# A fused attention and retrieval layer: probabilities scaled in place by ScalarE, Silu as one activation, and another order of the steady turn

## The reference

```python
scores = jnp.einsum('bhqd,bhkd->bhqk', qh, kh) * inv_sqrt_d
scores = jnp.where(causal, scores, jnp.finfo(scores.dtype).min)
attn = jax.nn.softmax(scores, axis=-1)
out = jnp.einsum('bhqk,bhkd->bhqd', attn, vh)
...
h = act(jnp.einsum('btd,cd->btc', hidden_states, W_up) + b_up)      # act is silu
h = jnp.einsum('btc,pc->btp', h, W_down) + b_down
q = jnp.einsum('btp,rp->btr', h, W_q)
...
sim = jnp.einsum('pbthn,hkpn->pbthk', q, keys)
scores, idx = lax.top_k(sim, K_PER_HEAD)
...
z = jnp.einsum('btd,bthkd->bthk', h, de)
z = act(z * jax.nn.softmax(sc, axis=-1))
out = jnp.einsum('bthk,bthkd->btd', z, ue)
...
x = x + jnp.tanh(g_xattn[0]) * _L0_xattn_ref(_layernorm(x, axis=-1), ...)
x = x + jnp.tanh(g_ffn[0]) * _L0_ffn_ref(_layernorm(x, axis=-1), ...)
```

## Time and profile before

| | |
|---|---|
| median of 3 executions | 1224.88 us (1223.29 to 1225.61) |
| the profiled execution, its own time | 1223.2 us |
| its span in the profile | 1221.5 us |
| TensorE matmuls busy | 1147.4 us, 94% |
| VectorE busy | 1074.5 us, 88% |
| ScalarE busy | 703.6 us, 58% |
| GpSimd busy | 332.6 us, 27% |
| mean granted TensorE clock | 0.98 |

### The profile page before, as it was taken

How to read it: one execution, slowest core, us unless ns; L and a number is a source line. 1 busy time by engine, 2 the same in 40 slices (tenths; PEclk the granted TensorE clock), 3 DMA queues, 4 the chain that set the end, 5 groups by cost and what they waited for, 6 DMA issues and landing times. The chain is left out here.

```text
span 1221.5 us, 47601 instructions
## 1 busy us (share of the span) xinstructions
PE 1147.4 (94%) x19004; PEld 1025.1 (84%) x19004; DVE 1074.5 (88%) x4298; ACT 703.6 (58%) x2474; POOL 332.6 (27%) x149
## 2 busy tenths in 40 slices
PE   6876999999999999999999999999999999999857
PEld 4766888888888888888889888888888888888856
DVE  3479999999999999999999999999999999998983
ACT  4656655556666555666556576655557665555310
POOL 4131233321233332123333212333321233331020
PEclk9987999999999999999999999999999999999978
DMA  8034655654565565456456435655644564654544
GB/s 220 12 102 116 151 110 124 151 130 120 125 151 111 123 151 128 115 132 148 101 135 151 128 115 132 151 87 146 151 122 119 135 151 87 147 144 114 127 120 79
DMA packets 304947, 154.52 MB, mean 127 GB/s; under 512 B 282735, under 2 KB 295895, under 8 KB 296535
## 3 DMA queue, kind: packets, MB, share of 16 engines
q1 hardware_dynamic: 304727, 151.47, 51.4%
HBM read 79.62 MB, written 4.72 MB: 69 GB/s over the span
## 5 line engine op out<-in xcount | busy, mean ns | idle before, releaser
L360 POOL TENSOR_TENSOR rstd<-veps,minus_half 128x1 f32<-128x1 f32 x32 | 67.9, 2123 | 709.9 <-DVE veps L831 709.9
L1162 PE MATMUL bank<-ue,coef 128*128 128x256 f32 x1024 | 228.5, 382 | 0.7 <-ACT coef L421 0.7
L1162 PEld LDWEIGHTS bank<-ue,coef 128*128 128x128 f32 x1024 | 193.5, 192 | 26.2 <-ACT coef L421 0.8
L928 PEld LDWEIGHTS bank<-z,hot_rT 128*128 128x128 bf16 x2048 | 155.7, 96 | 35.7 <-issue 23.1
L949 PE MATMUL bank<-uc,hot_r 128*128 128x32 bf16 x6144 | 162.0, 177 | 21.8 <-issue 16.8
L461 ACT ACTIVATE P<-bank,smax 128x64 f32<-128x64 f32 x512 | 152.2, 349 | 47.1 <-DVE smax L656 47.1
L949 PEld LDWEIGHTS bank<-uc,hot_r 128*128 128x128 bf16 x6144 | 158.0, 96 | 24.1 <-issue 20.4
L928 PE MATMUL bank<-z,hot_rT 128*128 128x32 bf16 x2048 | 164.9, 177 | 11.6 <-DVE picked L628 11.5
L928 PE MATMUL bank<-zl,hot_rT 128*128 128x32 bf16 x2048 | 163.7, 177 | 1.3 <-issue 1.2
L928 PE MATMUL bank<-zll,hot_rT 128*128 128x32 bf16 x2048 | 163.6, 177 | 0.0
L928 PEld LDWEIGHTS bank<-zl,hot_rT 128*128 128x128 bf16 x2048 | 156.5, 96 | 1.4 <-issue 1.3
(11 more groups left out here) (142 smaller groups left out, 2292.3 us busy)
## 6 DMA issues: line engine op xcount, KB each, us to landing
hot_rT<-expert_rows SPq DMA_DIRECT2D x64, 1024.0 KB, 6.2
xt<-in_x SPq DMA_DIRECT2D x32, 128.0 KB, 2.5
out<-x1k SPq DMA_DIRECT2D x32, 128.0 KB, 2.2
ct<-in_ctx SPq DMA_DIRECT2D x32, 64.0 KB, 2.3
ue<-in_L_ffn_up_embed SPq DMA_DIRECT2D x1, 2048.0 KB, 12.6
z<-in_L_ffn_W_up SPq DMA_DIRECT2D x1, 1024.0 KB, 8.0
expert_rows<-r_h SPq DMA_DIRECT2D x64, 8.0 KB, 1.8
hot_r<-hot_rT SPq DMA_TRANSPOSE x64, 6.9
```

What stands on the lines that cost most here:

```text
L360: nc.gpsimd.tensor_tensor(rstd[:, :], veps[:, :], minus_half[:, :], ALU.pow).then_inc(S["rstd_ok"], 1)
L928: last = mm(bank[:, 32 * (q - 16 * k):32 * (q - 16 * k) + 32], hot_rT[:, q, :], part.rearrange("r (h q) c -> r h q c", h=2)[:, :, q, :], s ...
L1162: last = mm(bG0[:, 0:DM], coef[:, c, :, :].rearrange("r h q -> r (h q)"), ue[:, c, :], start=(c == 0), stop=(c == C - 1))
```

## The change

Five things change together.

1. ScalarE scales the probabilities in place by `rinv`, with 16 new activations of 128x64 (`normed_probs`, L473). `r_wide`, its transpose and `rT` go, and `oT` becomes a plain copy (L821). The probabilities are transposed only after the scaling.
2. In steady turns Silu is one ScalarE activation with the bias in it (`up_silu`, L426), four of 128x128 per half. The tanh, and VectorE's product, go there. Silu is in another activation table than exp, so the built program has two table loads in each such turn.
3. In steady turns TensorE runs hidden layer, `dense(0)`, `dense(1)`, similarities and `dense(2)` ahead of the transposes of the probabilities, and the attended values behind `scatter(1)`. ScalarE's list follows.
4. The transposes of the normalised inputs move from the end of the products with the output rows to behind the 12th of the 16, those of the next tile's input with them.
5. The keys' two products use different rows and different banks, so `k_diag` is written by 8 activations of 128 columns and not by 4 of 256. VectorE's order of gather products, maxima and sums changes, and `dif` moves down a little.

The diff, cut to its core:

```diff
-                    WdT[:, 4 * g:4 * g + 4, :], 0.5
+                    WdT[:, 4 * g:4 * g + 4, :], 1.0
...
+                def up_silu(n):
+                    Fw.wait(f"up_pe{n}")
+                    Fw.free("hid_pe")
+                    for m in range(4):
+                        c = 4 * n + m
+                        last = nc.scalar.activation(up_act[:, c, :], bS[n][:, 128 * m:128 * m + 128], ACT.Silu,
+                                                    bias=bup_sb[:, c:c + 1])
+                    last.then_inc(S[f"act{n}"], 1)
...
                 def exps(half):
                     A.wait(f"max{half}")
-                    if Fw and Ct:
-                        Fw.wait("act1")
                     A.free("rinv_ok")
...
+                def normed_probs(half):
+                    for n in range(8):
+                        h = 8 * (n // 4) + 4 * half + n % 4
+                        last = nc.scalar.activation(P[:, h, :], P[:, h, :], ACT.Copy, scale=rinv[:, h:h + 1])
+                    last.then_inc(S[f"pn{half}"], 1)
...
                 if Fw and Ct:
-                    up_bias(0)
-                    up_tanh(0)
-                if B and Ct and not B.last:
-                    expert_exp(B)
+                    up_silu(0)
...
-                    for h in range(4):
-                        last = nc.scalar.activation(k_diag[:, :, :, h, :], bD[:, 256:512].rearrange("p (a b k) -> p a b k", a=2, b=2),
-                                                    ACT.Copy, scale=head_of[:, h:h + 1])
+                    for a in range(2):
+                        for h in range(4):
+                            last = nc.scalar.activation(k_diag[:, a, :, h, :], (bD, bT)[a][:, 384:512].rearrange("p (b k) -> p b k", b=2),
+                                                        ACT.Copy, scale=head_of[:, h:h + 1])
...
                 if Fw and Ct:
-                    up_bias(1)
-                    up_tanh(1)
+                    up_silu(1)
...
-                if A:
-                    probs_T(0)
-                    probs_T(1)
+                if A:
                     A.wait("rinv_ok")
-                    A.free("rT_pe")
-                    copy(r_wide[:, :, :], rinv[:, :].unsqueeze(2).to_broadcast([128, HEADS, HD]), "rw_ok")
+                    normed_probs(0)
+                    normed_probs(1)
...
-                if Fw:
+                if Fw and Ct:
                     z_copy(0)
                     z_copy(1)
-                if A:
-                    A.wait("rT_pe")
-                    A.free("o_ok")
-                    copy(rT[:, :, :], bD[:, 256:512].rearrange("d (a q) -> d a q", a=2), "rT_sb")
+                    similarities(0)
+                    similarities(1)
+                    z_copy(2)
+                if A:
+                    probs_T(0)
+                    probs_T(1)
...
-                if Fw and Ct:
-                    up_silu(0)
-                    up_silu(1)
                 if Ct:
                     gathered(0)
-                    gathered_sum(0)
                 if A and (Ct or not Fw):
                     scores_max(0)
+                if Ct:
+                    gathered(1)
+                if A and (Ct or not Fw):
                     scores_max(1)
                 if Ct:
-                    gathered(1)
+                    gathered_sum(0)
+                    gathered(2)
                     gathered_sum(1)
-                    gathered(2)
                     gathered(3)
...
                 if A:
-                    A.wait("rT_sb")
+                    A.wait("av_pe")
                     A.free("wo_pe")
-                    nc.vector.tensor_tensor(oT[:, :, :], bD[:, 0:256].rearrange("d (a q) -> d a q", a=2), rT[:, :, :], ALU.mult).then_inc(S["o_ok"], 1)
+                    nc.vector.tensor_copy(oT[:, :, :], bD[:, 0:256].rearrange("d (a q) -> d a q", a=2)).then_inc(S["o_ok"], 1)
...
                 def probs_T(n):
-                    A.wait(f"exp{n}")
+                    A.wait(f"pn{n}")
...
-                if A:
-                    probs_T(0)
+                if Fw:
+                    hidden()
+                if Fw and Ct:
+                    dense(0)
+                    dense(1)
+                    similarity(0)
+                    similarity(1)
+                    dense(2)
...
                 if Ct:
                     scatter(0)
                     scatter(1)
+                if A and Ct:
+                    attended()
+                if Ct:
                     scatter(2)
-                if Ct:
                     scatter(3)
...
                     for c in range(C):
+                        if c == 3 * C // 4:
+                            if A:
+                                normed_T()
+                            if L:
+                                inputs_T(L, 1 - side)
```

More of the change, by code:

```diff
@@ L548, in turn @@
                     exps(1)
-                if B and not Ct:
+                if B and not B.last:
                     expert_exp(B)
@@ L576, in turn @@
                         copy_weights(act, n)
-                if Fw:
+                if Fw and not Ct:
                     similarities(0)
@@ L1024, in output @@
                     last.then_inc(S["wo_pe"], 1)
-                if A:
-                    A.wait("xn_ok")
-                    A.wait_dma_side(f"ctx_in{side}")
-                    if Ct:
-                        Ct.wait("sm_ok")
-                    for k in range(2):
-                        nc.tensor.transpose(bT[:, 128 * k:128 * k + 128], xn1[:, 128 * k:128 * k + 128], ident[:, :])
-                    nc.tensor.transpose(bT[:, 256:384], ct[:, side, :, :].rearrange("p b d -> p (b d)"), ident[:, :]).then_inc(S["xT_pe"], 1)
+                if A and not Fw:
+                    inputs_T(A, side)
                 if Fw and Ct:
```

137 lines of the change are left out of this document (75 added, 62 removed), and 2 rows, old and new, of the table S.

## The result

The median of the changed kernel is 1392.37 us (1391.75 to 1392.47, 4 runs), against 1224.09 us (1221.12 to 1225.61) for the kernel before on the same chip. The ratio is 1.1381, with a 95% interval of 1.1361 to 1.1402. The direction and the ring of waits were forecast; the fall of TensorE's clock was not. The time lies 76 us above the forecast and 22 us above the end of the range.

A forecast was written before the change was run, and what follows sets the result against it. The prediction took TensorE as the bound before, VectorE close behind, and a ring through ScalarE after: 1223.2 us plus 84 for 29 steady turns at +2.9 plus 9 for the filling, 1316 us; full range 1270 to 1370.

The forecast's parts named there:

- the ring of waits: Chain from oT through VectorE, ScalarE and TensorE back to oT, six legs: 38.6 us a turn, 2.9 more than before.
- the fall of TensorE's clock: Rival, chance 0.02: TensorE waits about 4 us a turn, its clock halves, +2.2 us a turn, about 1380 us.
- the step that decides the sign: oT, ahead of VectorE's search, waits for attended values behind scatter(1); VectorE alone then takes 37.1 us a turn, over 35.74.
- VectorE's own 3.3 us of idle: VectorE's wait between uc and oT: two scatter groups 2.5, attended product 0.58, two hand-offs 0.2 us.
- leg 5: ScalarE from zt and hT 0.5 through 16 scalings 3.2 to the copies of z and sims 2.05: 5.75 us.
- leg 4: VectorE from gathered(1) through a maximum, gather products and sums to zp: 5.15 us.
- leg 6: TensorE's second half of transposed probabilities, two scatter groups, attended product and hand-off: 3.7 us.
- legs 1 to 3: VectorE from oT to topi 14.7, ScalarE from top_rep to Silu 6.8, TensorE's scores and gather(1) 2.5 us.
- My own range: The forecast's own range, 1288 to 1350 us, inside the full range of 1270 to 1370 us; the forecast had chance 0.77.
- The dear table load: Rival, chance 0.12: each ScalarE table load costs 2.6 us, not 1.28, adding 2.3 to the 38.6 us turn; 1383 us.
- The filling: The three turns of the filling with an A tile lengthen by 3 x 3.2, less r_wide and rT: +9 us.
- VectorE alone at 37.1 us a turn: VectorE's 35.5 less 1.7 plus 3.3 us, whatever ScalarE does; as a rival, chance 0.06, 1273 us.

The follow-up runs named there:

- experiment 3: Kernel before with the 16 scalings alone, other order as before: 1391.63 us; in a second run with the Silu activations and table loads alone: 1211.07 us.
- experiments 5 and 6: 2 of 16 scalings kept: changed kernel 1378.39 us, with oT behind the search 1272.34 us; with idle products in both TensorE waits 1339.41 us, all scalings there 1372.91 us.
- experiment 1: Changed kernel with 10 idle TensorE products in each steady turn, 8 ahead of the wait for k_diag and 2 within the mask: 1372.45 us.
- experiment 7: Changed kernel with oT behind the search, and GpSimd scaling all probabilities in one product: 1310.7 us; or with 10 idle TensorE products instead: 1367.53 us.

## Why the prediction was right, and where it was wrong

**What bounded before, and the sign: right.** TensorE was full and VectorE close behind. `oT` ahead of the search with its input behind `scatter(1)` was named as the step that decides the sign. It shows as a wait of 4.4 us in the mean, and moving that one copy gives back 102 us. But the search was not the only thing late: experiment 3 loses as much in the old order. What I called VectorE's own 3.3 us of idle is 3.4 us where the scalings are out of the way.

**The ring: right in its course, 1.4 us a turn too short.** This is a miss of size, and the largest. The forecast of 38.6 meets 40.0 us in a turn at full clock. No leg is far off. The scalings have a pitch of 0.24 us, not 0.20: (3.94 - 0.34) / 15. That is 0.6 us more than my term; leg 5 grows by 0.25 only, as the copies of `z` and `sims` behind them take 1.8 us and not 2.05. For the scaling I had taken the exponential without its accumulator read as the nearest row and gone to its lower end. The rest is 0.35 in leg 4, in the hand-offs and the small pauses between instructions on VectorE, 0.3 in leg 6 and 0.45 in legs 1 to 3 together. 29 turns of 1.4 us are 41 us. My own range ended at 1350, which allowed 1.2 us a turn for this; I had named 1.6 and called it rare.

**The price of an activation.** The trace gives 0.24 us for a scaling of 64 columns, and 0.26 for `k_diag` and Silu of 128, (2.20 - 0.36) / 7 and (1.14 - 0.37) / 3. The Trainium skill, "ScalarE: Activation LUTs", "What ACT_TABLE_LOAD costs", gives by its formula 0.24 and 0.29 for these, an estimate. It was right for the 64 columns, where I had no row, and too high for the 128, where I had one. With its price for the 64 columns leg 5 would have been 0.6 us longer, and the forecast nearer.

**The dear table load: out.** Load and next activation stand at 648.69 + 1.28 and 649.99, and `top_rep` ends where the load begins. Of all 60 loads of the turns none starts later than 0.02 us after the activation ahead of it, and the next activation starts 0.01 us behind the load where it waits for nothing else. The Trainium skill, "ScalarE: Activation LUTs", "What ACT_TABLE_LOAD costs", has 1.38 us of draining beside the 1.28; this trace shows none, at neither load of the turn. And the Silu half alone, which has the same two loads, makes the kernel faster. The ring at this rival's price, 40.9 us, and its time, 1383, come close to what was measured, but by chance.

**TensorE's clock: the step that failed.** I gave it a chance of 0.02, as a world of its own, and left it out of the forecast. It is no rival, it comes on top of the forecast ring: behind the wait for the keys the clock stands at 0.50 to 0.53 in the turn shown, the scores are as slow in 19 of 28 turns, and the falls add 0.9 us a turn in the mean, 26 us in all. I had priced it at 2.2 us, with scores, transposes and attended product all at half speed; in most turns only the scores are, 2.33 us in place of 1.26. That this rival's 1380 us lies near the measured time is chance: its clock was too dear and its ring too short. The forecast itself had TensorE wait in pieces of up to 1.5 us, and I left the clock at 1.00 because the trace of before showed no fall in a steady turn, which has no such waits. But the filling of the kernel before does have such waits, and its windows would have told me: from 90 to 120 us TensorE is busy 19.66 of 30 us, at a granted clock of 0.77. Two windows of the filling before, and one of the same stretch after:

```profile
30.00:60.00 30.00, 24.85 (x244) 21.22 (x243) 11.40 (x54) 19.69 (x74) 3.34 (x3) 1.00 0.05 14
...
90.00:120.00 30.00, 19.66 (x445) 17.02 (x442) 27.35 (x127) 18.85 (x68) 3.84 (x1) 0.77 0.50 129
```

```profile
30.00:60.00 30.00, 20.90 (x140) 17.30 (x139) 6.20 (x15) 20.98 (x84) 1.23 (x2) 0.78 0.03 7
```

**The filling: 9 us forecast, 21.6 measured.** The first `x1k` comes 26.8 us later, of which 5.2 are the one steady turn ahead of it. The scalings have 11 to 12 of these: 11.9 to 12.6 in experiments 5 and 6, less what they have in the one steady turn. That is more than the 9.6 of my term. The other 10 have no run of their own. The clock is lower there too, as the rows from 30 to 60 us show (0.78 against 1.00), and the hand-offs of the new order lie there; which of them it is stays open.

**The sum.** Forecast +93 us. 41 for the length of the ring, 26 for the clock and 13 for the filling make 173. The profiled execution came out 169 us above the one before (1392.47 against 1223.2): the emptying gives back 1, and the rest is rounding, 5.2 us a turn for a measured 5.13. Without the clock's 26 us the time would have been 1366, inside the range of 1270 to 1370; without the 41 too. With the filling's 13 alone put right it would still have been outside.

**VectorE alone at 37.1 us a turn: too low as a floor.** With the scalings all but gone and the clock up, the turn is still 39.43. That floor left out that VectorE waits 1.1 us for the scores and 0.6 for `gather(1)` behind them, which makes 38.8, where the shortest turns take 39.1. These waits hang on ScalarE's legs, which no free time on ScalarE removes.

**What I did not see at all** is that the change holds a gain. I costed Silu and its loads as legs of a ring, and never asked what they do without the ring: 0.990, and 0.981 with the early transposes.

## What to carry to other kernels

A copy of 0.42 us decided 102 us, because it stood ahead of the longest list of the fullest engine, and its input had been moved down. Before moving a producer, look at where its consumer stands in its engine's list and move it too. When a change makes TensorE wait in a turn, add a term for its clock to the likeliest case; it is not a separate event. And take a change apart before dropping it: here one half alone was 14% slower and another part 2% faster. Take the clock into account when a cut brings nothing: 14 scalings fewer were worth 0.8 us a turn and showed as nothing, since the clock fell more often.

## What the runs showed of the hardware that I had not expected

- A wait of 1.8 to 1.9 us ahead of the mask, in a turn in which TensorE is busy 36 of 41 us, is followed in 19 of 28 turns by scores at half speed; in the turn shown the clock is granted at 0.50 to 0.53 for some 6 us. The single turns of the same loop differ by this (40.0 to 41.8 us), since the fall does not come after each such wait. Behind the wait of 1.7 to 1.9 us for `hT` the 16 dense products took 2.05 us in 25 turns of the changed kernel and 3.5 to 3.7 in the other three.
- Filling one wait with idle products moved the fall to the next wait in 12 of 28 turns (experiment 1), and filling both kept the clock at 1.00 in nearly every turn. With all scalings it paid 20 us, with 2 of 16 it paid 39, and where TensorE had no such wait it cost what the products last.
- A table load has no pause at either end: `top_rep` ends at 648.68 and the load starts at 648.69, 1.28 long, with the next activation at 649.99.
- A VectorE product of 128x64 with two operands that starts beside GpSimd's product of 128x1024 lasts until that one ends: 1.90 us in place of 0.225 (experiment 7).
